# Six of 24 image quads convolved by pairs of rows with 12 taps instead of 18, and the rounding of the attention divided between two engines

## The reference

```python
for t in range(STEPS):                     # 3
    k = einsum('bhwc,cd->bhwd', x, Wk); v = einsum('bhwc,cd->bhwd', x, Wv)
    attn = softmax(einsum('nd,bsnd->bns', q, k) / sqrt(DIM_HEAD))
    pooled = einsum('bns,bsnd->bnd', attn, v); logits = pooled @ Wmlp
    weights = softmax(where(allowed > 0.5, logits, -1e9) / ROUTE_TEMP)
    wsel = the two largest of weights, normalised
    x_mod = x * (1.0 + attn.mean(heads) * S * softplus(alpha))
    y = sum_e wsel[:, e] * (conv3x3(x_mod, We[e]) + be[e])
    allowed = allowed without the top expert of each image (the last one stays)
    x = y
```

## Time and profile before

| what | value |
|---|---|
| median of 3 runs | 720.58 us (720.31 to 720.83) |
| profiled execution | 721.15 us |
| its span, first to last instruction | 719.3 us |
| PE busy | 682.1 us, 95% |
| PE weight loads | 274.0 us, 38% |
| DVE busy | 495.5 us, 69% |
| ACT busy | 277.0 us, 39% |
| POOL busy | 101.2 us, 14% |
| convolution matmuls (L551) | 380.9 us, 3456 records |

### The profile page before, as it was taken

The page is one execution under the profiler, slowest core; times in us unless marked ns, Lnnn a source line. Parts: engine busy times, 40 slices in busy tenths (PEclk is TensorE's granted clock), DMA queues, the critical chain, the costliest instruction groups (busy, mean ns, idle before and its releaser), DMA issues.

```text
span 719.3 us, 15066 instructions
## 1 busy us (share of the span) xinstructions
PE 682.1 (95%) x6464; PEld 274.0 (38%) x6464; DVE 495.5 (69%) x778; ACT 277.0 (39%) x368; POOL 101.2 (14%) x57
## 2 busy tenths in 40 slices
PE   7878999999999999999999999979999999999993
PEld 7433333333333333333333333324444444444432
DVE  5699758557545744674489679956877777777771
ACT  3763622222222222222200210034776776676642
POOL 2100100000000000000000300222342342342331
PEclk9999999999999999999999999998999999999997
DMA  9910000000000000000000000000111211211212
GB/s 330 198 41 1 2 1 2 1 1 2 1 1 2 1 2 1 1 2 1 1 12 3 1 2 1 1 1 1 31 31 30 59 31 30 59 31 30 59 31 58
DMA packets 54096, 19.68 MB, mean 27 GB/s; under 512 B 51123, under 2 KB 51861, under 8 KB 53909
## 3 DMA queue, kind: packets, MB, share of 16 engines
q1 hardware_dynamic: 53748, 18.57, 10.7%
q10 hardware_dynamic: 288, 0.21, 0.1%
HBM read 10.39 MB, written 8.39 MB: 26 GB/s over the span
## 4 chain that ended last, share of the span: by engine, by line
PE 84%; DVE 5%; issue 1%; ACT 1%; POOL 1%; DVEq 0%; POOLq 0%
PE conv L551 49%; PE conv L624 11%; PE att L641 10%; PE att L409 5%; PE att L590 4%; DVE x L1263 2%; PE att L602 2%; DVE stats L1074 1%; PE att L467 1%; PE att L612 1%; DVE comb L1060 1%; DVE xpad L1025 0%; POOL x L1329 0%; POOL rstack L1322 0%; ACT x L848 0%
## 5 line engine op out<-in xcount | busy, mean ns | idle before, releaser
L551 PE MATMUL conv<-xpad,comb 64*64 64x512 f32 x3456 | 380.9, 591 | 0.1
L551 PEld LDWEIGHTS conv<-xpad,comb 64*64 64x64 f32 x3456 | 129.5, 133 | 224.0 <-issue 218.3
L1263 DVE TENSOR_TENSOR x<-conv,x 128x1024 f32<-128x1024 f32 x144 | 170.3, 1220 | 50.1 <-PE conv L624 49.8
L1060 DVE SCALAR_TENSOR_TENSOR comb<-experts,wsel,comb 128x576 f32<-128x576 f32 x138 | 102.6, 812 | 57.6 <-ACT comb L739 57.6
L624 PE MATMUL conv<-rstack,wse 98*128 98x512 f32 x288 | 102.0, 460 | 5.8 <-POOL rstack L1322 2.6
L749 ACT ACTIVATE x<-conv,bias 128x512 f32<-128x512 f32 x64 | 40.4, 682 | 158.8 <-PE conv L551 158.7
L641 PE MATMUL att<-x,sum_sel 64*32 64x512 f32 x1280 | 80.4, 600 | 0.0
L1025 DVE SCALAR_TENSOR_TENSOR xpad<-att,x 128x1024 f32<-128x1024 f32 x46 | 54.1, 1219 | 32.9 <-PE att L467 32.9
L624 PEld LDWEIGHTS conv<-rstack,wse 98*128 98x128 f32 x288 | 48.0, 193 | 70.9 <-DVE x L1263 35.5
L739 ACT ACTIVATE comb<-experts,wsel 128x576 f32<-128x576 f32 (+1 forms) x52 | 35.2, 732 | 79.7 <-PE conv L551 75.2
L1329 POOL TENSOR_TENSOR x<-x,xin 128x1024 f32<-128x1024 f32 x16 | 38.3, 2394 | 132.7 <-ACT x L848 132.7
(11 more groups left out here) (137 smaller groups left out, 411.3 us busy)
## 6 DMA issues: line engine op xcount, KB each, us to landing
x<-in_x SPq DMA_DIRECT2D x32, 256.0 KB, 5.2
out<-comb SPq DMA_DIRECT2D x32, 256.0 KB, 3.2
experts<-in_We SPq DMA_DIRECT2D x1, 1152.0 KB
wide<-in_c_wide SPq DMA_DIRECT2D x1, 192.0 KB, 5.6
x<-in_c_sum SPq DMA_DIRECT2D x1, 160.0 KB
small<-in_c_small ACTq DMA_DIRECT2D x1, 142.5 KB, 3.6
map_sel<-in_c_map SPq DMA_DIRECT2D x1, 128.0 KB
wr<-in_Wr SPq DMA_DIRECT2D x6, 4.0 KB
```

Of the source, the lines that this page charges most:

```text
L551: last = nc.tensor.matmul(conv[own[to], h, HW * rows:HW * rows + HW], comb[own[rows], q % 2, n, t * C:t * C + C], xpad[own[rows], 2 * (q % ...
L1060: v.scalar_tensor_tensor(comb[:, q % 2, n, :], experts[:, e, :], wsel[:, p % 2, j + QP * n, e:e + 1], comb[:, q % 2, n, :], ALU.mult, ALU. ...
L1263: v.tensor_tensor(img(prod[i]), img(conv[:, unit, :]), xip[s][:, kh:kh + H, kw:kw + W], ALU.mult)\
```

## The change

Quads 4, 6, 8, 10, 12 and 14 (j = 0 and 2 of phases 1, 2 and 3; `SHORT`) are convolved by F(2,3) along the rows: two output rows are made from four products instead of six. With the filter's rows g0, g1, g2 and the padded input rows d0 to d3 the products are (d1 + d2) by (g0 + g1 + g2)/2, (d2 - d1) by (g0 - g1 + g2)/2, (d0 - d2) by g0 and (d1 - d3) by g2. The first two, added and subtracted, are the middle of both output rows; the third is added to the upper row and the fourth subtracted from the lower one. Each product is a stage of three taps over 16 rows of 32 pixels for all images of the quad, so a quad has 12 taps and not 18.

- **POOL.** Once, `row_forms` makes the half sum of the filter rows for each expert as a fourth column block of `experts`. For each short quad `subtract_rows` makes the other combined form (two instructions of 192 columns), and then, in place in `xpad`, the two row differences (1,088 elements each).
- **DVE.** `combine` of a short quad has 768 columns, not 576. `sum_rows` adds and subtracts neighbouring rows (two instructions of 1,088 elements) after `modulate`. `middle_rows` (two of 1,024) makes the middles of both output rows, and `finish_rows` (two of 1,024, one after each of the last stages) completes them and frees PSUM. A small memset renews the border row that the differences overwrote.
- **ACT.** `copy_middle` (two of 512) takes the place of the four instructions of `empty_conv`. For phases 2 to 5 `round_attention` scales the attention and makes its three bf16 roundings; `reduce_attention` on DVE keeps the two subtractions between them. `scale_attention` and `split` remain for phases 0 and 1, and `parts` has one buffer, not two.
- **PE.** The matmuls beside the taps move: attention after the first tap of a short quad j = 0 (in phase 1 with `permute(1)` ahead of it), `logits` to the second tap of quad j = 1, the map to later taps, `permute` to j = 3.
- Small tiles are shared or cut to make room; the experts' rows are stored in the order middle, upper, lower.

The core of the diff:

```diff
+SHORT = tuple(QP * p + j for p in range(1, LAST) for j in (0, 2))
+ROW = 3 * C
+ROW_AT = (1, 0, 2)
...
-        experts = sb("experts", [128, K, TAPS * C])
-        comb = sb("comb", [128, 2, 2, TAPS * C])
+        experts = sb("experts", [128, K, 4 * ROW])
+        comb = sb("comb", [128, 2, 2, 4 * ROW])
+        cmp = sb("cmp", [128, 3, GP, K, K])
+        parts = sb("parts", [128, S], BF16)
+        row_sums = sb("row_sums", [128, 2, 2, H // 2, PW])
...
+        def emptied(eng, q, h):
+
+            if q in SHORT:
+                eng.wait_ge(short_emptied, 2 * SHORT.index(q) + h + 1)
+            else:
+                eng.wait_ge(conv_emptied, 2 * (sections(q, h) - 2 * sum(s < q for s in SHORT)))
+
+        def tap(t):
+
+            kh, kw = divmod(t, 3)
+            first = ROW_AT[kh] * ROW + kw * C
+            return slice(first, first + C)
+
+        def rows_of(q, h):
+
+            first = slot(q, 0)
+            return x[:, first:first + QP + 1:QP, :].rearrange("p n (r e c) -> p n r e c", e=2, c=W)[:, :, :, h, :]
...
-                    eng.wait_ge(conv_emptied, 2 * sections(QP * (p - 1) - 1, 1))
+                    emptied(eng, QP * (p - 1) - 1, 1)
+                    if p > 2:
+                        emptied(eng, QP * (p - 2) + 1, 1)
...
@@ -513,11 +553,11 @@
                         attend(p + 1, "values", uw)
                     elif at == (0, 1, 2):
                         attention_map(q + 1)
-                    elif at == (0, 1, 7):
+                    elif at == (1, 0, 1):
                         logits(p + 1)
-                    elif at in ((1, 0, 3), (2, 0, 3), (3, 0, 3)):
+                    elif at in ((1, 0, 5), (2, 0, 3), (3, 1, 2)):
                         attention_map(q + 1)
-                    elif at == (2, 1, 4):
+                    elif at == (3, 0, 5):
                         permute(p + 1)
...
+            def beside_short(p, j, at):
+                q = QP * p + j
+                if j == 0 and at == (0, 0):
+                    if p == 1:
+                        permute(1)
+                    attend(p + 1, "scores", sw)
+                    attend(p + 1, "values", uw)
+                elif at == ((2, 0) if j == 0 else (1, 1)):
+                    attention_map(q + 1)
+
+            def convolve_short(p, j):
+
+                q, w = QP * p + j, SHORT.index(QP * p + j)
+                odd = [xpad[:, 2 * (q % 2) + n, 1:H + 1:2, :] for n in range(2)]
+                even = [xpad[:, 2 * (q % 2) + n, 0:H:2, :] for n in range(2)]
+                stages = ((0, 3, [row_sums[:, 0, n, :, :] for n in range(2)]), (1, 0, [row_sums[:, 1, n, :, :] for n in range(2)]),
+                          (0, 1, even), (1, 2, odd))
+                for n in range(2):
+                    eng.wait_ge(comb_added[n], (K - 1) * (2 + q + 1))
+                for m, (h, form, rows_in) in enumerate(stages):
+                    if m < 2:
+                        emptied(eng, q - 1, h)
+                        eng.wait_ge(sums_ready, 2 * w + m + 1)
+                        if m:
+                            eng.wait_ge(minus_ready, 2 * (w + 1))
+                    else:
+                        eng.wait_ge(differences_ready, 2 * w + m - 1)
+                        eng.wait_ge(middle_read if h else middle_copied, 2 * (w + 1))
+                    for kw in range(3):
+                        for n, rows, to in ((0, 0, 0), (1, 0, 1), (1, 1, 0), (0, 1, 1)):
+                            last = nc.tensor.matmul(
+                                conv[own[to], h, HW * rows:HW * rows + HW],
+                                comb[own[rows], q % 2, n, form * ROW + kw * C:form * ROW + kw * C + C],
+                                rows_in[n][own[rows], :, kw:kw + W], start=(kw == 0), stop=(kw == 2))
+                        if kw == 2:
+                            last.then_inc(middle_full if m < 2 else conv_full, 1)
+                        else:
+                            beside_short(p, j, (m, kw))
...
                 q = QP * p + j
                 before = sections(q, h) - 2
                 if before > 0:
                     if before <= 2 * QP * LAST:
-                        eng.wait_ge(conv_emptied, 2 * before)
+                        emptied(eng, q - 1, h)
+                if q - 2 in SHORT and h == 0:
+                    eng.wait_ge(edge_cleared, SHORT.index(q - 2) + 1)
...
+                if q in SHORT:
+                    eng.wait_ge(forms_ready, 3)
+                    taps = [slice(0, 4 * ROW)]
...
+            def copy_middle(q):
+
+                p, j = divmod(q, QP)
+                if j == 0:
+                    eng.wait_ge(bias_ready, p + 1)
+                eng.wait_ge(middle_full, 2 * SHORT.index(q) + 1)
+                for n in range(2):
+                    nc.scalar.activation(rows_of(q, 1)[:, n, :, :],
+                                         conv[:, 0, n * HW:(n + 1) * HW].rearrange("p (r c) -> p r c", c=W),
+                                         ACT.Identity, bias=bias[:, p % 2, n, j:j + 1]).then_inc(middle_copied, 1)
+
+            def round_attention(p, n):
+
+                if n == 0:
+                    eng.wait_ge(scale_ready, p - 1)
+                    nc.scalar.activation(attn[:, :], attn[:, :], ACT.Copy, scale=soft[:, 6:7]).then_inc(attn_ready, 1)
+                    eng.wait_ge(attn_ready, p)
+                    for m in range(2):
+                        use = Use("map", QP * p - 1, m)
+                        eng.wait_ge(att_full[use.unit], use.full)
+                else:
+                    eng.wait_ge(reduced, 2 * (p - 2) + n)
+                nc.scalar.activation(parts[:, :], attn[:, :], ACT.Copy).then_inc(parts_ready if n == 2 else rounded, 1)
...
                         begin_combine(q + 1)
                     if p < PHASES - 1 and j == 0:
                         exponentials(p + 1)
+                    if q in SHORT:
+                        copy_middle(q)
                     if p < PHASES - 1 and j == 1:
                         route_exp(p + 1)
-                    if p < LAST:
+                    if p < PHASES - 1 and j == 2:
+                        round_attention(p + 1, 0)
+                    if p < PHASES - 1 and j == 3:
+                        round_attention(p + 1, 1)
+                        round_attention(p + 1, 2)
+                    if p < LAST and q not in SHORT:
                         for h in range(2):
                             empty_conv(q, h)
...
+                if q - 2 in SHORT:
+                    v.memset(xpad[:, 2 * (q % 2):2 * (q % 2) + 2, 0, :], 0.0).then_inc(edge_cleared, 1)
...
+            def sum_rows(q):
+
+                w = SHORT.index(q)
+                pads = xpad[:, 2 * (q % 2):2 * (q % 2) + 2, :, :]
+                modulated(eng, q)
+                if w:
+                    eng.wait_ge(middle_full, 2 * w)
+                v.tensor_tensor(row_sums[:, 0, :, :, :], pads[:, :, 1:H + 1:2, :], pads[:, :, 2:H + 2:2, :], ALU.add)\
+                    .then_inc(sums_ready, 1)
+                v.tensor_tensor(row_sums[:, 1, :, :, :], pads[:, :, 2:H + 2:2, :], pads[:, :, 1:H + 1:2, :], ALU.subtract)\
+                    .then_inc(sums_ready, 1)
+
+            def middle_rows(q):
+
+                eng.wait_ge(middle_full, 2 * SHORT.index(q) + 2)
+                eng.wait_ge(middle_copied, 2 * SHORT.index(q) + 2)
+                both = conv[:, 1, :].rearrange("p (n r c) -> p n r c", n=2, c=W)
+                v.tensor_tensor(rows_of(q, 0), rows_of(q, 1), both, ALU.add).then_inc(middle_read, 1)
+                v.tensor_tensor(rows_of(q, 1), rows_of(q, 1), both, ALU.subtract).then_inc(middle_read, 1)
+                eng.wait_ge(middle_read, 2 * SHORT.index(q) + 2)
+
+            def finish_rows(q, h):
+
+                eng.wait_ge(conv_full, sections(q, h))
+                both = conv[:, h, :].rearrange("p (n r c) -> p n r c", n=2, c=W)
+                v.tensor_tensor(rows_of(q, h), rows_of(q, h), both, ALU.subtract if h else ALU.add).then_inc(short_emptied, 1)
+
+            def reduce_attention(p, n):
+
+                eng.wait_ge(rounded, 2 * (p - 2) + n + 1)
+                v.scalar_tensor_tensor(attn[:, :], parts[:, :], below[:, n:n + 1], attn[:, :], ALU.mult, ALU.add).then_inc(reduced, 1)
+
             def combine(q):
                 p, j = divmod(q, QP)
+                cols = slice(0, 4 * ROW if q in SHORT else TAPS * C)
...
             modulate(4)
+            sum_rows(4)
             next_mask_and_bias(1)
 
             for p in range(1, PHASES):
@@ -1218,6 +1377,10 @@
                         permuted(1)
                     if q - 1 >= QP * LAST:
                         final(q - 1, 1)
+                    if q - 1 in SHORT:
+                        finish_rows(q - 1, 1)
+                    if j == 3 and attended:
+                        reduce_attention(p + 1, 0)
                     if q + 1 < QUADS:
                         if j == 1 and attended:
```

(43 more changed lines are left out.)

80 lines of the change are left out of this document (48 added, 32 removed).

## The result

The changed kernel takes 722.44 us (median of 10 runs, 721.42 to 725.09); the kernel before, measured beside it, took 720.36. The ratio is 1.0035 (95% interval 1.0023 to 1.0048): slower by 0.35%, where 702.4 and faster had been predicted. The profiled execution has a span of 719.9 us against 719.3.

The account below looks back on a forecast made before the run. PE bounds the kernel, with no stall to give back. Saving 30.9 us, less 3.2 at entry, 3 x 2.75 and 2 x 0.55 in stalls and 0.1 for roundings, leaves 18.2: 720.58 becomes 702.4, range 699.0 to 710.0.

Parts of the forecast that it names:

- PE's side of the ledger: Six short quads lose 6 taps each on PE: 36 taps at 0.858 us, a ceiling of 30.9 us saved.
- rival 5: Short quads' taps: reading every second row of `xpad` halves PE's rate in half the stages; about 721 us, chance 0.03.
- Rival 2: DVE dearer in the short quads, through strided rows, waits between dependent steps or port sharing; 709.7 us, chance 0.19.
- rival 1: DVE cheaper than listed or overlapping more, removing both stalls in C: 695.8 us, half of it 699; chance 0.12.
- the paragraph on GpSimd: POOL's differences, 2.5 us each, stay hidden by slack even at twice the price; POOL gives way and DVE does not.
- The slower rival: VectorE waits for GpSimd wherever they run side by side: 15.3 us in C, 11.4 in A; 729 us, chance 0.04.
- C: Quad j = 2 of a phase, short, the tight place: PE stalls 1.15 us before the fourth stage; DVE never idles.
- A: Quad j = 0 of a phase, short, beginning with the attention: last stage ends at 16.9 us, middle rows wait for PE.
- B: Quad j = 1 of a phase, 18 taps: runs from 17.4 to 33.7 us after PE waits 0.55 for its first half.
- the entry: Entering phase 1, before quad 4: PE waits for sums and mask, attention starts at 132.5 not 129.3, 3.2 us lost once.
- D: Quad j = 3 of a phase: PE waits 1.05 us, starts it at 46.7 and ends it at 62.95 us.
- Rival 3: PE's clock falls to 1.2 GHz in the stalls, at least 1.9 us at phase 1's entry; 704.3 to 706.2, chance 0.05.

## Why the prediction was wrong, point by point

- **PE's side of the ledger held.** The convolution's records went from 3,456 to 2,592 and 576, at 4.52 us for five taps. Strided reads cost nothing, so rival 5 falls.
- **VectorE's prices held.** Combine of 768 columns took 5.66 for six, as written; the sums 1.29 and 1.28, middle rows 2.4 for two, `finish_rows` 2.34 for two, the memset 0.12. Rival 2 falls, and rival 1 gains little: 64.28 against 64.4 in the kernel with the differences cut.
- **The step that failed is the paragraph on GpSimd**: "So POOL gives way and DVE does not". From rows 8 I had taken that in a meeting of the two it is POOL that is lengthened (1.02 to 1.51), and from rows 9 that combine never is. Both rows are true, and both show one case only: DVE's combine was already running when POOL's instruction, of four elements, came. Further combines did start before that instruction ended, and took their 0.81, but four elements are no test of 1,088. No row of before had VectorE arriving while a long POOL instruction ran. Where it does, VectorE waits for its end: 0.18 became 2.49, and six combines 8.71 us instead of 4.46.
- **The Trainium skill had the rule.** The Trainium skill, page SBUF — State Buffer (Who interferes with whom), says that the port pair that VectorE and GpSimd share goes for a whole instruction to whoever issues first, and that `tensor_reduce` and instructions with at most one SBUF input outside the two-port modes don't contend. The trace agrees: 2.49 beside 2.5, the reduction at 0.19, the PSUM readers at 1.22; one meeting under the small form below does not follow the order. Read with it, rows 8 shows the other order of arrival. The prediction had drawn on the line of the Trainium skill's GPSIMD Engine Reference (Specifications) that says only "contention", and let a row overrule it that didn't bear on the case.
- **The slower rival had the mechanism, at a chance of 0.04, and a wrong size.** Its price was 729 against 722.4 measured. It charged 5.1 us in C (measured: 2.34 + 2.05 = 4.39) and 3.8 in A (measured: combine longer by 2.5, but B starts 17.9 after the attention, not 17.5 as with the differences cut, so 0.4), and nothing at the entry, where the wait costs 4.6. From the start of the attention, in phase 2:

| | forecast | differences cut | after |
|---|---|---|---|
| B starts | 17.4 | 17.5 | 17.9 |
| C starts | 33.7 | 34.0 | 37.7 |
| D starts | 46.7 | 46.5 | 51.2 |
| next attention | 64.4 | 64.3 | 69.0 |

- **The sum that should have stood there.** Attention of phase 1 at 137.6 and not 132.5: 5.1, of which 4.6 are the two stretched instructions. Three phases by 4.4: 13.2. The scores at the lowered clock: 1.5. That is 19.8, against the 20.0 by which the median missed 702.4 and the 18.8 by which the profiled execution, from which these terms are read, missed 703.0. About 1 of the last difference lies behind the short quads, where the kernel after is faster: from the last attention to the end it takes 373.4 us, the kernel before 374.3. "Nobody waiting for them" was looked for in PE's waits on POOL, of which there are indeed none; the cost came in by way of VectorE.
- **Rival 3, the clock, came true as an addition.** The scores at the entry took 5.14 us after, 5.34 with the differences cut. But it is no fixed price: that kernel's waits of 1.38 and 0.95 stood as 1.41 and 0.95 in the kernel that holds POOL back, and there the scores took 3.64; and with one stall of 2.04 the clock from 132 to 136 was 0.60, 0.64 and 0.65 in three kernels and 1.00 in a fourth. In C, phase 2, the first five taps took 6.22 for 4.52 and cost nothing, since VectorE was late there anyway: the wait of 1.53 ahead of the fourth stage, seen in phase 1, is gone in phase 2, and D's stays 0.58.
- **The small form** (192 columns) took 1.11 each where I had 0.65, and here POOL is the one that waits. The first of a pair starts while the last combine still runs (125.54 and 125.38 us) and takes 1.30; the second takes 0.59, as I had it, beside modulate, which reads PSUM. Where a two-input instruction of DVE comes between the two, both sides lose, DVE 1.61 for 1.27 and POOL 1.57 for 0.59; the cost was hidden as said:

```profile
196.78 2.84 POOL L1487 TENSOR_TENSOR comb<-comb 128x192 f32<-128x192 f32 x2 [22.10 <-DVE comb L1218]
197.55 1.61 DVE L1207 SCALAR_TENSOR_TENSOR attn<-parts,small,attn 128x1024 f32<-128x1024 bf16 x1
```

  Who came first by the trace doesn't settle every meeting. In the kernel that holds POOL back, the same DVE instruction started 0.76 us behind POOL's, which was still waiting for the combine; it was not stretched, and POOL's two took 3.06 us. Why it went ahead there is open:

```profile
189.00 3.06 POOL L1487 TENSOR_TENSOR comb<-comb 128x192 f32<-128x192 f32 x2 [10.22 <-DVE comb L1218]
189.76 1.28 DVE L1207 SCALAR_TENSOR_TENSOR attn<-parts,small,attn 128x1024 f32<-128x1024 bf16 x1
```

## What to carry to other kernels

Before you hand work to GpSimd, list which VectorE instructions will run in its window and where their inputs lie: in these traces those with both inputs in SBUF stood still until the POOL instruction ended (one with a single SBUF input did too, L1124), and those that read PSUM and the reductions didn't. If the cheap engine takes twice as long and the busy one is blocked meanwhile, leave the work where it is: here 2.5 us on VectorE were worth 5.0 on POOL, and that alone turned 722.4 into 714.3. And a row that shows A waiting for B in one order of arrival says nothing of the other order; a tiny instruction in the way is no test for a long one.

## What the runs showed that was not expected

- For a VectorE instruction that comes just behind it, the length of a POOL instruction is the length of the stop, to 0.1 us, with one input (copy, 1.07 us for 1,088 elements) as with two (2.5 us). The copy ran at over twice the pace of the subtraction.
- Instructions of 24 to 32 elements are the ones hurt most in proportion (0.18 to 2.5), and they sit at the heads of chains to ACT and PE.
- PE's granted clock was 0.50 in the four us that hold the end of a wait of 5.54 us, and 0.58 in those behind one of 3.66, while the same wait of 3.66 in phase 1 of that kernel lowered nothing. Why the same stalls gave 0.60 to 0.65 at the entry in three kernels and 1.00 in a fourth stays open. It also blurs comparisons of the variants: 1 to 1.7 us on the scores alone.
